# A mixture-of-experts block: the experts' first bias moves from a TensorE product to a VectorE addition

## The reference

```
x = x + attention(layernorm(x))                       # x: 16 x 512 x 256
t = layernorm(x) as 8192 x 256
shared = gelu(t @ sw1 + sb1) @ sw2 + sb2
probs = softmax(t @ gate_w + gate_b)                  # 8 experts
combine = the two largest probs of each token, zero elsewhere
h = gelu(t @ w1[e] + b1[e])                           # w1[e]: 256 x 256, b1[e]: 256
y = h @ w2[e] + b2[e]
x = x + sum over e of combine[:, e] * y[e] + shared
```

## Time and profile before

| what | value |
|---|---|
| median of 3 runs | 2104.12 us (2102.28 to 2105.59) |
| the profiled execution's own time | 2105.01 us |
| its span in the profile | 2102.2 us |
| PE busy | 1975.4 us, 94% |
| DVE busy | 1697.7 us, 81% |
| ACT busy | 1417.6 us, 67% |
| POOL busy | 1037.6 us, 49% |
| DMA, mean over the span | 53 GB/s |

### The profile page before, as it was taken

The page is one execution under the profiler, slowest core; times in us unless marked ns, Lnnn a source line. Parts: engine busy times, 40 slices in busy tenths (PEclk is TensorE's granted clock), DMA queues, the critical chain, the costliest instruction groups (busy, mean ns, idle before and its releaser), DMA issues.

```text
span 2102.2 us, 35982 instructions
## 1 busy us (share of the span) xinstructions
PE 1975.4 (94%) x12605; PEld 1557.8 (74%) x12605; DVE 1697.7 (81%) x2867; ACT 1417.6 (67%) x2170; POOL 1037.6 (49%) x1204
## 2 busy tenths in 40 slices
PE   6899999999999999999999999999999783999998
PEld 4577777777777777777777777777777562999998
DVE  6678888888888888888888888898988886565565
ACT  6678686868686868686868686868686651444444
POOL 3435454545454545454555555554545453344344
PEclk9999999999999999999999999999999996999999
DMA  4000101010101010101010101010101024764664
GB/s 130 1 21 1 51 1 51 1 51 1 51 1 51 1 51 1 51 1 51 1 51 1 51 1 51 1 51 1 51 1 41 1 71 128 227 190 134 190 183 140
DMA packets 73649, 112.24 MB, mean 53 GB/s; under 512 B 9716, under 2 KB 52219, under 8 KB 73477
## 3 DMA queue, kind: packets, MB, share of 16 engines
q1 hardware_dynamic: 58468, 67.86, 11.4%
q0 software_dynamic: 15008, 42.10, 5.4%
HBM read 63.10 MB, written 48.65 MB: 53 GB/s over the span
## 4 chain that ended last, share of the span: by engine, by line
PE 72%; DVE 15%; ACT 8%; issue 3%; DMA 1%; POOL 0%; SPq 0%; POOLq 0%; DVEq 0%
PE bank_o L1181 10%; PE ring L1161 6%; PE ring L1140 6%; PE ring L1088 5%; PE ring L1166 5%; PE ring L1089 5%; PE ring L1094 5%; DVE norm L766 3%; ACT prob L557 3%; PE bank_d L1192 3%; PE ring L1147 3%; ACT prob L563 2%; PE acc L1201 2%; DVE kT L752 2%; DVE q_lo L757 2%
## 5 line engine op out<-in xcount | busy, mean ns | idle before, releaser
L557 ACT ACTIVATE prob<-ring 128x1024 f32<-128x1024 f32 (+1 forms) x384 | 327.0, 877 | 223.3 <-PE ring L1166 219.6
L766 DVE RECIPROCAL norm<-bank_d 128x512 f32<-128x512 f32 x128 | 429.5, 3356 | 26.8 <-PE bank_d L1192 25.0
L483 POOL TENSOR_SCALAR_AFFINE_SELECT prob<-prob 128x256 f32<-128x256 f32 x512 | 220.0, 450 | 447.5 <-ACT prob L563 447.5
L494 POOL TENSOR_TENSOR key_sum<-prob 128x768 f32<-128x768 f32 x128 | 241.3, 1885 | 345.0 <-PE bank_d L1192 338.2
L563 ACT ACTIVATE prob<-prob 128x1024 f32<-128x1024 f32 (+1 forms) x384 | 344.3, 915 | 5.2
L1181 PE MATMUL bank_o<-prob,v 128*64 128x512 f32 (+3 forms) x2048 | 308.4, 444 | 18.6 <-DVE norm L768 18.6
L752 DVE TENSOR_TENSOR kT<-ring,kT 64x512 fp32r<-64x512 f32 x256 | 176.3, 689 | 124.6 <-ACT kT L570 120.9
L1161 PE MATMUL ring<-qT,kT 128*128 128x256 f32 (+3 forms) x1024 | 239.2, 335 | 32.2 <-DVE xnTl L739 11.8
L1181 PEld LDWEIGHTS bank_o<-prob,v 128*64 128x64 f32 x2048 | 128.2, 138 | 177.3 <-issue 154.9
L1161 PEld LDWEIGHTS ring<-qT,kT 128*128 128x128 f32 x1024 | 165.5, 189 | 110.1 <-issue 50.5
L1166 PE MATMUL ring<-q_lo,kT 128*128 128x256 f32 (+3 forms) x1024 | 225.5, 322 | 0.4 <-DVE q_lo L757 0.4
(11 more groups left out here) (222 smaller groups left out, 4766.6 us busy)
## 6 DMA issues: line engine op xcount, KB each, us to landing
xin<-first SPq DMA_DIRECT2D x71, 257.0 KB, 3.3
xin<-second SPq DMA_DIRECT2D x71, 129.0 KB, 2.7
xin<-base SPq DMA_DIRECT2D x71, 128.0 KB, 2.8
x_next<-in_x SPq DMA_DIRECT2D x16, 512.0 KB, 3.8
x_res<-in_x SPq DMA_DIRECT2D x16, 512.0 KB, 3.8
raw_e<-in_w SPq DMA_DIRECT2D x4, 1024.0 KB, 7.1
first<-pad SPq DMA_DIRECT2D x9, 257.0 KB, 4.8
second<-pad SPq DMA_DIRECT2D x9, 129.0 KB, 5.7
```

Source lines behind the costliest of these rows:

```text
L483: last = nc.gpsimd.affine_select(out=diag, in_=diag, compare_op=ALU.is_ge, fill=0.0, base=0, pattern=[[0, 2], [1, P]], channel_multiplier=-1)
L494: nc.gpsimd.tensor_tensor(key_sum[:, :, :], t0[:, :, P:N], t13[:, :, 0:N - P], ALU.add).then_inc(sum_steps, 1)
L557: nc.scalar.activation(probs[p % 2][u][:, :, :], slot[:, :, 0:UNIT_COLS[u]], ACT.Tanh, scale=SCALE / SOFTCLAMP).then_inc(act_emptied, 1)
L766: nc.vector.reciprocal(norm[:, :], bank_d[:, :]).then_inc(o_steps, 1)
```

## The change

The first layer's bias is no longer a product. DVE adds it while it moves the sums from `ring[0]` into a new tile `act_in` in SBUF (`add_bias`), from a copy of all eight biases that stands in every partition (`b1_all`, 128 x 2048, loaded by one DMA), at an offset from a register. ACT takes gelu of `act_in` in place of `ring[0]`. The second bias stays a product.

```
-                    sp.dma_start(b_raw, b1_twice[:, 0:E * D // 2]).then_inc(bias_loaded, 16)
+                    sp.dma_start(b_raw, b2_twice[:, 0:E * D // 2]).then_inc(bias_loaded, 16)
...
             sp.wait_ge(projected, NSEQ * PAIRS)
+            sp.dma_start(b1_all[:, :], b1_row[0, :].partition_broadcast(P)).then_inc(bias1_loaded, 16)
             load_experts(1, raw_e2, w2)
...
             def activate(n):
-                act.wait_ge(h_full, n + 1)
+                act.wait_ge(h_biased, n + 1)
                 if n >= 2:
                     act.wait_ge(h_turned, n - 1)
-                nc.scalar.activation(act_out[n % 2][:, :], ring[0][:, n % 2, 0:FF], ACT.Gelu).then_inc(h_done, 1)
+                nc.scalar.activation(act_out[n % 2][:, :], act_in[n % 2][:, :], ACT.Gelu).then_inc(h_done, 1)
...
-                    if i == NSEQ - 1 and p in (0, 1, 2, 3):
+                    if i == NSEQ - 1 and p in (0, 1):
                         prepare_bias(p)
...
+            def add_bias(n):
+                if TILE[n][1] % BATCH == 0:
+                    weights_of(mybir.EngineType.DVE, n, bias_at)
+                dve.wait_ge(h_full, n + 1)
+                if n >= 2:
+                    dve.wait_ge(h_done, n - 1)
+                nc.vector.tensor_tensor(act_in[n % 2][:, :], ring[0][:, n % 2, 0:FF],
+                                        b1_all[:, bass.ds(bias_at[n], D)], ALU.add).then_inc(h_biased, 1)
...
             count = len(TILE)
+            dve.wait_ge(bias1_loaded, 16)
             in_low(0)
             in_low(1)
+            add_bias(0)
             for n in range(count):
                 if n + 2 < count:
                     in_low(n + 2)
+                if n + 1 < count:
+                    add_bias(n + 1)
                 act_low(n)
                 if n >= 1:
                     weigh(n - 1)
...
-                pe.matmul(dst, ones_r[:, :], biases[:, bass.ds(at, D)], start=False, stop=False)
+                if biases is not None:
+                    pe.matmul(dst, ones_r[:, :], biases[:, bass.ds(at, D)], start=False, stop=False)
...
                 if n >= 2:
-                    pe.wait_ge(h_done, n - 1)
-                expert_product(ring[0][:, n % 2, 0:FF], xinT[n % 2], w_e1, b_rows[0], weights_at_tile[n],
+                    pe.wait_ge(h_biased, n - 1)
+                expert_product(ring[0][:, n % 2, 0:FF], xinT[n % 2], w_e1, None, weights_at_tile[n],
                                (in_lo, n + 1)).then_inc(h_full, 1)
```

More of the change, by code:

```diff
@@ L109, in block_program @@
 def block_program(nc, x, wqT, wkT, wvT, woT, gate_w, gate_b_rows, w1s, w1, w2s, w2,
-                  b1s_cols, sb2_twice, b1_twice, b2_twice, out):
+                  b1s_cols, sb2_twice, b1_row, b2_twice, out):
     first = nc.dram_tensor("first", (ROWS, FIRST_ROW), F32).ap()
@@ L167, in block_program @@
         table_call = sb("table_call", [P, 1])
-        b_rows = [sb(f"b{k}_rows", [P, E * D], F32R) for k in (1, 2)]
+        b2_rows = sb("b2_rows", [P, E * D], F32R)
         pad = sb("pad", [P, FIRST_ROW])
@@ L217, in block_program @@
             y_out = [sb(f"y_out{k}", [P, D], F32, arena) for k in range(YOUT)]
+            act_in = [sb(f"act_in{k}", [P, FF], F32, arena) for k in range(2)]
+            b1_all = sb("b1_all", [P, E * D], F32, arena)
         head_rows = [slice(0, DH), slice(DH, P)]
@@ L267, in block_program @@
         bias_loaded = sem("bias_loaded")
+        bias1_loaded = sem("bias1_loaded")
         pad_ready = sem("pad_ready")
@@ L283, in block_program @@
         h_full = sem("h_full")
+        h_biased = sem("h_biased")
         h_done = sem("h_done")
@@ L318, in block_program, with weights_of @@
         TILE = tile_list()
+        def weights_of(engine, n, known):
+            k, j = TILE[n]
+            starts_at = nc.values_load_multi_w_load_instructions(
+                table[K + k:K + k + 1, j:j + BATCH], engines=(engine,), min_val=0, max_val=(E - 1) * D,
+                skip_runtime_bounds_check_because="an expert's number below 8 times 256, or zero")[1]
+            known.update({n + m: at for m, at in enumerate(starts_at) if j + m < TILES})
         BIAS_STEPS = 5
@@ L347, in _ @@
                 sp.dma_start(x_res[:, :, :], x_tiles[i]).then_inc(xres_loaded, 16)
[L349 to L352, removed]
+            sp.wait_ge(bias_steps, BIAS_STEPS + 4)
+            sp.dma_start(b_raw, b2_twice[:, E * D // 2:]).then_inc(bias_loaded, 16)
             def load_experts(k, dst, src):
@@ L446, in _ @@
                            channel_multiplier=0).then_inc(pad_ready, 1)
-            for k in range(K):
-                nc.gpsimd.memset(b_rows[k][:, :].bitcast(F32), 0.0)
+            nc.gpsimd.memset(b2_rows[:, :].bitcast(F32), 0.0)
             nc.gpsimd.iota(taken[:, :, 0, :], [[0, K], [REGION, E]], base=0, channel_multiplier=0,
@@ L922, in prepare_bias @@
             def prepare_bias(n):
-                k, half = n // 2, slice(n % 2 * E * D // 2, (n % 2 + 1) * E * D // 2)
-                row, steps = b_rows[k][0:K, half], BIAS_STEPS + 4 * n
+                half = slice(n * E * D // 2, (n + 1) * E * D // 2)
+                row, steps = b2_rows[0:K, half], BIAS_STEPS + 4 * n
                 dve.wait_ge(bias_loaded, 16 * (n + 1))
@@ L1057, in act_low @@
                                         actT[n % 2][0][:, :, :].bitcast(F32), ALU.subtract).then_inc(act_lo, 1)
+            bias_at = {}
+            def add_bias(n):
[6 more added lines that the diff above has]
+                                        b1_all[:, bass.ds(bias_at[n], D)], ALU.add).then_inc(h_biased, 1)
             def weigh(n):
+                dve.wait_ge(y_full, n + 1)
                 k, j = TILE[n]
-                dve.wait_ge(y_full, n + 1)
                 if k == 1:
@@ L1350, in _ @@
             weights_at_tile = {}
[L1352 to L1359, removed]
             def expert_hidden(n):
                 if TILE[n][1] % BATCH == 0:
-                    load_weights_of(n)
+                    weights_of(mybir.EngineType.PE, n, weights_at_tile)
                 pe.wait_ge(in_hi, n + 1)
                 if n >= 2:
-                    pe.wait_ge(h_done, n - 1)
-                expert_product(ring[0][:, n % 2, 0:FF], xinT[n % 2], w_e1, b_rows[0], weights_at_tile[n],
+                    pe.wait_ge(h_biased, n - 1)
+                expert_product(ring[0][:, n % 2, 0:FF], xinT[n % 2], w_e1, None, weights_at_tile[n],
                                (in_lo, n + 1)).then_inc(h_full, 1)
@@ L1382, in expert_out @@
                     pe.wait_ge(y_ready, n - 1)
-                expert_product(acc[:, n % 2, 0:D], actT[n % 2], w_e2, b_rows[1], weights_at_tile[n],
+                expert_product(acc[:, n % 2, 0:D], actT[n % 2], w_e2, b2_rows, weights_at_tile[n],
                                (act_lo, n + 1)).then_inc(y_full, 1)
@@ L1387, in _ @@
             pe.wait_ge(e_lo, 8)
-            pe.wait_ge(bias_steps, BIAS_STEPS + 16)
+            pe.wait_ge(bias_steps, BIAS_STEPS + 8)
             pe.wait_ge(table_ready, 1)
@@ L1432 @@
         "sb2_twice": twice(L0_ffn_sb2),
-        "b1_twice": twice(L0_ffn_b1),
+        "b1_row": laid(np.asarray(L0_ffn_b1).reshape(1, -1)),
         "b2_twice": twice(L0_ffn_b2),
```

## The result

| what | before | after |
|---|---|---|
| median | 2105.4 us (8 runs, 2102.28 to 2106.76) | 2111.14 us (8 runs, 2107.83 to 2112.29) |
| ratio, 95% interval | | 1.0027 [1.0016, 1.0038] |
| profiled execution's own time, span | 2105.01, 2102.2 us | 2111.53, 2109.8 us |
| first product of the tiles' stage | 1785.89 us | 1774.90 us |
| length of that stage (span less that start) | 316.3 us | 334.9 us |

The kernel got slower by 5.7 us, 0.27%. I had forecast 20 us. The profiles show two parts of opposite sign: the tiles' stage takes 18.6 us more, and it begins 11.0 us earlier.

What follows compares the result with a forecast made beforehand. PE bounds the kernel before; afterwards a DVE-ACT ring of 2.32 us a tile was to set the pace. 2105.0 - 12 + 31.5 + 1 = 2125.5 us, less 0.9 for the median, given as 2125; range 2108 to 2162.

Steps and rivals of the forecast that it cites:

- The gain of the product: Tiles' stage, PE: one of 18 products goes, 0.12 us x 142 = 17 us, if PE still sets the pace.
- a ring of DVE and ACT: Tiles' stage: addition, gelu, act_high, act_low and on to the next addition form a 2.32 us loop; +31.5 us.
- Rival (a): Tiles' stage: PE stays the bound at 1.975 us a tile, the ring being shorter; 2076 us; chance 0.08.
- the notice from DVE to ACT: Tiles' stage: time from the addition's end to gelu's start on ACT, taken as 0.08 us.
- my lower bound: Tiles' stage: ring of 2.25 us, with a notice of 0.05 and nothing for gelu's new source; +21.7 us.
- The 1 us for the beginning and end of the halves: Each half's ends: a tile's way is longer by addition and notice (0.5 us), shorter by a product; +1 us.
- the last sequence: First stage's end: bias instructions at p = 2 and 3 leave DVE, so PE waits less; -12 us.
- Rival (d): Last sequence: it gives nothing, because the next engine is late there; 2137 us; chance 0.10.
- the 2.2 us that I had counted for the clock: Last sequence: PE's time lost at clock 0.72 in the 8 us after its longest gap, regained; 2.2 us.
- the zeros: Register instruction, loads of eight numbers, PE's changed wait, the new 1 MB DMA and POOL's memset: each zero.
- Rival (b): Tiles' stage: DVE's operations don't overlap, or the register instruction shows; ring 2.45 to 2.80 us; chance 0.15.
- Rival (c): Tiles' stage: PE's clock falls because PE idles; +60 us if a third of tiles, 2185 us; chance 0.05.

Runs made afterwards that it cites:

- swap_act: Kernel after with act_high(n) moved ahead of activate(n+1) in ACT's list, all work the same; 2077.98 us.
- product_back: Kernel after with an 18th product per tile put back on PE, the second bias' rows standing in; 2114.67 us.
- extra_add: Kernel after with a second, unused addition per tile on DVE, into a spare tile ahead of the real one; 2159.56 us.
- swap_extra: swap_act with a second, unused addition per tile on DVE, into a spare tile; 2084.74 us.
- after_again: Kernel after, unchanged, measured again on the same chip; 2111.53 us.
- fixed_offset: Kernel after with expert 0's bias added for every tile, without DVE's register instruction and loads of eight numbers; 2109.77 us.
- gelu_psum: Kernel after with gelu reading ring[0] in PSUM, still waiting for the addition, and PE waiting for gelu; 2109.63 us.
- before_swap: Kernel before with act_high(n) moved ahead of activate(n+1) in ACT's list; 2108.53 us.
- prepare_four: Kernel after with DVE again preparing the bias at p = 2 and 3 of the last sequence (second bias twice); 2125.87 us.
- swap_hold: swap_act with DVE's splits of the experts' weights waiting until the last scattering transfer into first has landed; ratio to before 0.9862.
- swap_late: swap_act with the bias preparations at p = 0 and 1 moved behind the last sequence; 2068.81 us.

## Why the prediction was off in size and right in kind

**Right: the bound.** The gain of the product is lost whole, in a ring of DVE and ACT that one turn of the lists must go round. swap_act opens it and shows 33 us between closed and open; product_back shows that PE has slack in it; extra_add against swap_extra shows that the same operation of DVE costs some seven times as much inside it (eleven times by the stage's length). Rival (a), PE stays the bound at 1.975 us a tile and 2076 us, did not come, but it had named its own condition (gelu not ahead of `act_high`), and where that was made true the kernel took 2077.98 us.

**Failed: the size of the ring, above all the notice from DVE to ACT.** The sum 0.43 + 0.08 + 0.33 + 0.36 + 0.04 + 0.34 + 0.40 + 0.34 = 2.32 us was 0.09 too long. From the rows of the timelines after:

| step | forecast | measured |
|---|---|---|
| addition to gelu (addition 0.43, notice 0.08) | 0.51 | 0.45 (1840.30 to 1840.75) |
| gelu to `act_high` | 0.33 | 0.33 |
| `act_high` to `act_low` (0.36, notice 0.04) | 0.40 | 0.38 |
| `act_low` to `weigh` | 0.34 | 0.34 |
| `weigh` to `in_low` | 0.40 | 0.39 |
| `in_low` to the next addition | 0.34 | 0.34 |
| turn | 2.32 | 2.23 |

The largest error is the notice from DVE to ACT. I took 0.08 between 0.10 and 0.05, and it is 0.03 to 0.04; the addition is 0.01 shorter, `act_high` and its notice 0.02. Even my lower bound (2.25 us, +21.7) was above what came. The error is 4% of the ring, but what costs is the ring less the 2.095 us of before, 0.225 forecast and 0.133 measured: 31.5 us against (2.228 - 2.095) x 140 = 18.6 us, which is the stage's growth in the profiles. These 13 us are nearly the whole miss of 14, and they are why I forecast +20 us where +5.7 came. The 1 us for the beginning and end of the halves did not show.

**Right: the last sequence.** I took -12 us. One pair of profiles gives -11.0, but that reading scatters by some 2 us. Over the eight profiles with the preparations at p = 0 and 1 alone (after, after_again, swap_act, extra_add, swap_extra, product_back, fixed_offset, gelu_psum) the stage starts at 1774.0 on average, over the three with four of them (before, before_swap, prepare_four) at 1786.3: -12.3 us. So with 18.6 the sum is +6.3 us, beside 5.7 measured. Rival (d), that nothing is gained there, falls with prepare_four. In the clock I had one thing wrong. The dip to 0.72 behind the 6.33 us wait is gone, but there is now one earlier, at 1640 to 1656 us, of 8 x (0.15 + 0.06) = 1.7 us:

```profile
1640.00:1648.00 8.00, 6.06 (x29) 3.49 (x29) 7.78 (x9) 5.92 (x9) 5.88 (x7) 0.85 0.00 0
1648.00:1656.00 8.00, 8.00 (x49) 6.48 (x46) 7.87 (x8) 5.73 (x8) 6.22 (x8) 0.94 0.00 0
```

PE's wait of 1.94 us at 1644.60 lies in it; the kernel before had the same wait half a microsecond earlier with the clock at 1.00, so what made the difference is open. It is not the change: after_again, the same kernel as after, has the wait too (1.92 us) and the clock stays at 1.00, and its stage starts 1.3 us later all the same. So the 2.2 us that I had counted for the clock can't be seen above the scatter of this reading, and that -12 was met does not bear them out; to that extent it was luck.

**Right: the zeros.** Register instruction and loads cost 0.8 us in the whole stage (fixed_offset), the new transfer and PE's changed wait nothing that shows. Rival (b) did not come: DVE's operations start 0.33 to 0.39 us apart in the ring, 0.07 to 0.09 us before the one in front ends, although each has a wait of its own, so the first reading of the rule in the Trainium skill ("VectorE: DVE Perf Modes", "The DRAIN you can't avoid"), 2.56 us a turn, is not what happens; its second sentence, that an operation which is not held starts earlier, agrees. Rival (c) did not come either: PE has 0.25 us to spare in each turn, and the granted clock stays at 1.00 in the windows read of the stage. The swing that the page "TensorE: Matmul & The Clock Gate" of the Trainium skill, section "A second HAM failure mode: psum-queue depth-cycling", tells of is not seen in them.

## What to carry to other kernels

An operation put on an engine with time to spare still costs its whole start-to-start distance when it closes a loop between two in-order lists: write down who waits for whom in one turn and add up the loop before looking at busy shares. If the loop is longer than the bound, look first for a swap in one list that opens it; here one swapped pair of calls was worth 33 us, six times what the change had cost. And when two paces lie close together, the price is their difference: an error of 4% in one was 40% of the price, so such a forecast needs the handovers at the same pair of engines and the same shape of operation, or a wider range.

## What the runs showed of the hardware

- POOL's issue of an indirect transfer stands still while DVE runs operations with two inputs from SBUF: 9.65 us in place of 0.98, while DVE's eight splits of 128x1024 run, and 0.98 again once they are moved (swap_hold). The "GPSIMD Engine Reference" of the Trainium skill, section "Specifications", says that POOL's way to SBUF is shared with VectorE and contended by instructions with two SBUF inputs, which agrees. DVE's operations of the tiles' stage do not do it: POOL's transfers there take 0.97 us, however DVE is loaded. Those have one input from PSUM, and are also shorter (0.42 to 0.48 us against 1.15); no run separates the two.
- That stall can be put where nobody waits. In swap_late DVE starts its splits behind POOL's transfers into `first`, and it is a transfer into `second` that is stretched to 10.81 us, needed only in the second half.
- A load of eight numbers into DVE's registers adds 0.03 us to its turn in the kernel after, where DVE waits for ACT anyway, and leaves DVE idle for 0.4 to 0.8 us in swap_act, where it does not. A wait for ACT alone does not cover it: extra_add has the same 0.74 us of it, and most of its turns with a load are 0.2 to 0.3 us longer.
- With 384 products started in 50 us in place of 432, PE's granted clock stayed at 1.00 in the windows read of the stage, the upper of its two levels (2.4 GHz). In extra_add it is 333 in 50 us, and 1.00 too. One wait of PE of 1.9 us in the last sequence went with 0.85 in one profile of the kernel after and with 1.00 in the other.
